# A recurrent layer's group norm without its mean: value weight and first states centred once, and the instruction order of four engines rewritten

## What is computed

```python
xa = _ln(x, ln1_w, ln1_b)
...
r = (xr @ Wr.T).reshape(b, l, h, s_)
k = (xk @ Wk.T).reshape(b, l, h, s_)
v = (xv @ Wv.T).reshape(b, l, h, s_)
g = jax.nn.silu(xg @ Wg.T)
s0 = state[:, 2:2 + s_].reshape(b, h, s_, s_)

def step(s, rkvw):
    r_t, k_t, v_t, w_t = rkvw
    a = k_t[..., :, None] * v_t[..., None, :]
    out = jnp.einsum('bhi,bhij->bhj', r_t, u * a + s)
    s = a + w_t[..., :, None] * s
    return (s, out)
...
og = out.reshape(b, l, h, s_)
m = og.mean(-1, keepdims=True)
va = ((og - m) ** 2).mean(-1, keepdims=True)
og = ((og - m) / jnp.sqrt(va + 1e-05)).reshape(b, l, e) * gn_w + gn_b
x1 = x + og * g @ Wo.T
xc = _ln(x1, ln2_w, ln2_b)
...
return x1 + rr * (kk @ Wfv.T)
```

## Time and profile before

| | |
|---|---|
| median of 3 runs | 4187.91 us (4187.29 to 4189.38) |
| the profiled execution | 4184.89 us, span 4183.2 us |
| the second layer in its span | first load issued at 648.59, last product of the output 1618.31 to 1619.00 |
| first scan, last scan | 727.78 and 1546.4 us |
| one sample in the steady part | 105.8 us, from the start of one variance matmul (L1222) to the next: 946.94, 1052.77, 1158.60, 1264.40, 1370.20 |
| busy in such a stretch | PE 104.20, PEld 78.30, DVE 93.23, ACT 32.80, POOL 63.76 us |
| granted clock of TensorE in it | 1.00 |

### The profile page before, as it was taken

How to read it: one execution, slowest core, us unless ns; L and a number is a source line. 1 busy time by engine, 2 the same in 40 slices (tenths; PEclk the granted TensorE clock), 3 DMA queues, 4 the chain that set the end, 5 groups by cost and what they waited for, 6 DMA issues and landing times. The chain is left out here.

```text
span 4183.2 us, 68211 instructions
## 1 busy us (share of the span) xinstructions
PE 3942.0 (94%) x20652; PEld 2981.3 (71%) x20652; DVE 2936.5 (70%) x6449; ACT 1925.5 (46%) x3836; POOL 1598.0 (38%) x1100
## 2 busy tenths in 40 slices
PE   7999996799999987999999999999999999999989
PEld 3333334567777755888977888877988877978866
DVE  6766652888888874767767767757767757767653
ACT  4666661233333323555543555533545534555522
POOL 1443432555666641332344332344332344333240
PEclk8999997999999998999999999999999999999999
DMA  5444423000000002222223222223121122122122
GB/s 169 127 129 131 132 61 127 11 6 16 16 16 16 11 11 84 72 66 77 64 66 109 62 75 72 64 74 104 58 90 57 61 79 90 61 92 70 54 79 98
DMA packets 159993, 298.64 MB, mean 71 GB/s; under 512 B 19780, under 2 KB 42820, under 8 KB 158544
## 3 DMA queue, kind: packets, MB, share of 16 engines
q1 hardware_dynamic: 157720, 291.12, 22.4%
q0 software_dynamic: 1008, 3.67, 0.2%
q10 hardware_dynamic: 1032, 0.97, 0.1%
HBM read 254.28 MB, written 42.21 MB: 71 GB/s over the span
## 5 line engine op out<-in xcount | busy, mean ns | idle before, releaser
L2220 POOL TENSOR_TENSOR c_wl<-c_wr,c_wh 128x512 fp32r<-128x512 f32 (+1 forms) x576 | 820.0, 1435 | 1606.1 <-ACT c_wh L2600 1368.1
L2701 ACT ACTIVATE c_pr<-c_ps,c_nms 128x257 f32<-128x257 f32 x512 | 244.2, 477 | 475.4 <-DVE c_nms L2940 473.1
L1741 DVE TENSOR_TENSOR_SCAN b_sb<-b_wt,b_s,b_ps 128x256 f32<-128x256 f32 x512 | 361.7, 736 | 15.6 <-PE b_ps L1194 3.1
L843 DVE TENSOR_REDUCE a_nm<-a_ps 128x2 f32<-128x1024 f32 x256 | 312.0, 1223 | 69.1 <-PE a_ps L490 68.4
L1692 POOL TENSOR_TENSOR b_sb<-b_sb,b_rt 128x1024 f32<-128x1024 f32 x128 | 277.8, 2177 | 156.2 <-DVE b_sb L1741 115.9
L2600 ACT ACTIVATE c_wh<-c_wr 128x512 fp32r<-128x512 f32 (+1 forms) x464 | 315.5, 688 | 45.8 <-PE c_ps L2307 41.9
L686 ACT ACTIVATE a_ex<-a_ps 128x1024 f32<-128x1024 f32 x256 | 260.6, 1022 | 147.2 <-PE a_ps L510 145.0
L2305 PE MATMUL c_ps<-c_hh,c_wh 128*128 128x512 f32 x768 | 307.4, 400 | 7.3 <-DVE c_hl L2806 7.3
L2305 PE MATMUL c_ps<-c_gh,c_wh 128*128 128x512 f32 x768 | 307.5, 400 | 6.2 <-DVE c_gl L3003 2.9
L2307 PE MATMUL c_ps<-c_hh,c_wl 128*128 128x512 f32 x768 | 304.4, 396 | 0.0
L2306 PE MATMUL c_ps<-c_hl,c_wh 128*128 128x512 f32 x768 | 304.1, 396 | 0.0
(11 more groups left out here) (379 smaller groups left out, 9985.4 us busy)
## 6 DMA issues: line engine op xcount, KB each, us to landing
c_wr<-in_downs SPq DMA_DIRECT2D x192, 256.0 KB, 2.6
c_wr<-in_wv SPq DMA_DIRECT2D x64, 512.0 KB, 4.0
c_wr<-in_wk SPq DMA_DIRECT2D x128, 256.0 KB, 2.9
c_wr<-in_wq SPq DMA_DIRECT2D x128, 256.0 KB, 2.6
a_qp<-strips SPq DMA_DIRECT2D x64, 256.0 KB, 4.5
a_kp<-strips SPq DMA_DIRECT2D x64, 256.0 KB, 4.5
c_wr<-in_fc SPq DMA_DIRECT2D x64, 256.0 KB, 2.8
strips<-a_qh SPq DMA_DIRECT2D x32, 256.0 KB
```

The lines of the kernel that those rows point to most:

```text
L843: dve.tensor_reduce(NM[:, s, :].rearrange("p (h c) -> p h c", h=HG)[:, 2 * p:2 * p + 2, c:c + 1], ps[:, bank:bank + 2, :], AX.X, ALU.max, ...
L1741: mm = dve.tensor_tensor_scan(SB[:, quad % RING, pr % 2, e, 1:L + 1], WT[:, third(b, i), e, :], half(spread_bank(pair), e), S0[:, b % 2, 2 ...
L2220: pool.tensor_tensor(piece(WL, slot), piece(WR, slot), piece(WH, slot), ALU.subtract).then_inc(piece_cut[slot], 1)
L2701: act.activation(PR[:, i, 0:L + 1], ps[:, BS + 1 - i % 2, 0:L + 1], ACT.Exp, bias=NMS[:, i:i + 1], scale=float(K2) ** -0.5, accum_out=RS[: ...
```

## The change

The weights of v and the first states get their mean over j taken out once, in the prologue, by VectorE (`center`); then `out` has no mean over j, and the two mean matmul groups, their subtractions, `BM` and the semaphores between them go, in the steady part and in the tail. The square now waits for the scans' sums themselves (`og_ready`). `S0` is loaded whole, for all 8 samples, by one transfer of 256 KB ahead of the later weights, in place of eight of 32 KB. The four tables are other ones throughout, and the products have a slot each.

```diff
-            for dst, src in ((SELF, selv), (SELG[:, :, :], selg), (BO[:, 0, :], blk[0]), (BM[:, :], blk[1]), (BMC[:, :, :], bmc), (BB[:, :, :], bb)):
+            for dst, src in ((SELF, selv), (SELG[:, :, :], selg), (BO[:, 0, :], blk), (BMC[:, :, :], bmc), (BB[:, :, :], bb)):
                 sp.dma_start(dst, src).then_inc(consts_in, 16)
-            sp.dma_start(S0[:, 0], s0[0]).then_inc(s0_in[0], 16)
+            sp.dma_start(S0[:, :, :, :], s0).then_inc(s0_in, 16)
...
-                    if t > 1:
-                        sp.wait_ge(s_ready, (t - 1) * PAIRS1 + AHEAD)
-                        sp.wait_ge(first_in, (t - 1) * QUADS + AHEAD)
-                    sp.dma_start(S0[:, t % 2], s0[t]).then_inc(s0_in[t % 2], 16)
...
                                 if t == 0:
-                                    pe.wait_ge(weights_in[w], 16)
+                                    if w == W_V:
+                                        pe.wait_ge(wv_centered, 1 + AHEAD)
+                                    else:
+                                        pe.wait_ge(weights_in[w], 16)
...
-                for i in range(2):
-                    s = due_post(slot, PE_AT["gm"][i])
-                    if s is not None:
-                        pe.wait_ge(og_ready, s * 2 + i + 1 + AHEAD)
-                        if i == 0:
-                            pe.wait_ge(fv_read, s * 2 + AHEAD)
-                        else:
-                            pe.wait_ge(gc_ready, s * 2 + 1 + AHEAD)
-                        for c in range(2 * i, 2 * i + 2):
-                            mm = pe.matmul(half(PB, c), BM[:, :], OG[:, s % 2, c, :], start=True, stop=True, skip_group_check=True)
-                        mm.then_inc(gm_ps, 1)
                 s = due_post(slot, PE_AT["gv"])
                 if s is not None:
                     pe.wait_ge(gq_ready, s + 1 + AHEAD)
-                    pe.wait_ge(gc_ready, s * 2 + 2 + AHEAD)
+                    pe.wait_ge(fv_read, s * 2 + AHEAD)
...
-                    act.wait_ge(gc_ready, s * 2 + 2 + AHEAD)
+                    act.wait_ge(og_ready, s * 2 + 2 + AHEAD)
...
+            def center():
+
+                dve.wait_ge(s0_in, 16 + AHEAD)
+                states = S0[:, :, :, :].rearrange("p b c j -> p (b c) j")
+                dve.tensor_reduce(SDB[:, 0:B * EC], states, AX.X, ALU.add)
+                dve.drain()
+                dve.scalar_tensor_tensor(states, SDB[:, 0:B * EC].unsqueeze(2).broadcast_to([P, B * EC, S1]), -1.0 / S1, states, ALU.mult, ALU.add).then_inc(s0_centered, 1)
+                dve.wait_ge(weights_in[W_V], 16)
+                sums = SDB[:, P:2 * P].rearrange("p (c h) -> p c h", h=HC1)
+                dve.tensor_reduce(sums, W[:, W_V].rearrange("p k (o j h) -> p (k o) h j", o=EC, h=HC1), AX.X, ALU.add)
+                dve.drain()
+                dve.tensor_scalar(sums, sums, 1.0 / S1, None, ALU.mult)
+                dve.drain()
+                columns = W[:, W_V].rearrange("p k (o j h) -> p (k o) j h", o=EC, h=HC1)
+                dve.tensor_tensor(columns, columns, sums.unsqueeze(2).broadcast_to([P, EC * EC, S1, HC1]), ALU.subtract).then_inc(wv_centered, 1)
...
+                            if t == 0 and e == 2 and i == 0:
+                                center()
...
-                for i in range(2):
-                    s = due_post(slot, DVE_AT["gm"][i])
-                    if s is not None:
-                        dve.wait_ge(gm_ps, s * 2 + i + 1 + AHEAD)
-                        dve.tensor_tensor(OG[:, s % 2, 2 * i:2 * i + 2, :], OG[:, s % 2, 2 * i:2 * i + 2, :],
-                                          both(PB), ALU.subtract).then_inc(gc_ready, 1)
...
-                    b = due(slot, 4 * pr + DVE_AT["multiply"])
+                    b = due(slot, DVE_AT["multiply"][pr])
```

More of the change, by code:

```diff
@@ L1099, in layer1 @@
         U_K, U_R, U_TW1, U_TW2, U_BONUS, U_V, U_G, UNITS = 0, 2, 4, 5, 7, 9, 11, 13
[L1100 to L1109, removed]
-                       mix=(-123, -121, -104, -71, -57), rk=(-111, -100), gate=-39, gated=143, scale2=166, shift2=188)
@@ L1111, in layer1 @@
-        DVE_AT = dict(multiply=-1, sums=(79, 148), mean=-111, inverse=-102, blend=-92, mix=(-81, -78, -73, -70, -56, -53, -42, -35, -29, -22),
-                      v=(-19, -11), gm=(168, 171), ginverse=182, bb=(184, 186), wo=(203, 209), mean2=213, inverse2=219, fkin=234, frin=239,
-                      fv=(283, 292), out=312)
-        FIRST, LAST = -188, B * SLOTS + 320
+        PE_AT = dict(mean=-158, var=-155, hidden=-122, mix=(-119, -114, -109, -102, -97, -92, -71, -66, -64, -61), k=(-105, -99), r=(-96, -86),
+                     tw1=-75, tw2=(-70, -65), bonus=(-64, -62), v=(-57, -51), g=(-46, -43),
+                     spread=(-46, -45, -43, -41, -39, -38, -32, -26, -23, -13, -5, 5, 6, 9, 12, 14, 18, 20, 29, 30, 34, 39, 40, 46, 53, 58, 63, 71, 72, 75, 76, 80),
+                     gather=(-12, 6, 15, 41, 58, 65, 83, 95), gv=137, bb=(148, 152), wo=(161, 168), mean2=169, var2=180, fk=(203, 207),
+                     fr=(219, 228), fv=(243, 253))
@@ new lines, in layer1 @@
+        ACT_AT = dict(square=-133, root=-111, norm=-106, hidden=-104, k=(-82, -70), r=(-69, -51), tw1=-47, tw2=(-46, -44), bonus=(-43, -42),
+                      v=(-40, -37), g=(-31, -16), states=(-14, -13, 10, 12, 21, 35, 47, 48, 58, 59, 61, 76, 82, 92, 93, 94), gsquare=147, groot=174,
+                      gnorm=175, square2=193, root2=207, norm2=214, fk=(217, 231), fr=(242, 256))
+        POOL_AT = dict(scale=-181, shift=-178, mix=(-162, -157, -126, -105, -98), rk=(-127, -106), gate=-73,
+                       weigh=(-69, -68, -58, -51, -42, -40, -2, 0, 1, 3, 19, 23, 31, 32, 34, 44), gated=113, scale2=149, shift2=158)
@@ L1116, in layer1 @@
+        DVE_AT = dict(mean=-109, inverse=-100, blend=-87, mix=(-76, -74, -73, -68, -62, -50, -33, -31, -28, -25), v=(-20, -12),
+                      multiply=(-4, -1, 4, 9, 12, 14, 17, 27, 29, 30, 33, 43, 44, 49, 56, 58, 62, 63, 64, 75, 76, 79, 80, 90, 96, 98, 99, 106, 110, 115, 116, 123),
+                      sums=(86, 150), ginverse=183, bb=(184, 187), wo=(202, 207), mean2=211, inverse2=218, fkin=233, frin=237, fv=(286, 299), out=311)
+        FIRST, LAST = -189, B * SLOTS + 320
         stack.callback(nc.all_engine_barrier)
@@ L1389, in last_stages @@
                 pe.wait_ge(mix_read, B * 10 + AHEAD)
-                for i in range(2):
-                    pe.wait_ge(og_ready, s * 2 + i + 1 + AHEAD)
-                    for c in range(2 * i, 2 * i + 2):
-                        mm = pe.matmul(half(LAST_BANKS[i], c), BM[:, :], OG[:, s % 2, c, :], start=True, stop=True, skip_group_check=True)
-                    mm.then_inc(gm_ps, 1)
                 pe.wait_ge(tr_ready, r * 2 + 1 + AHEAD)
```

36 lines of the change are left out of this document (14 added, 22 removed).

## The result

The changed kernel takes 4237.69 us (median of 4 runs, 4231.16 to 4238.75) against 4187.6 before: ratio 1.0118, 95% interval 1.0106 to 1.0131. It is slower by 50 us. The profiled execution has a span of 4237.2 us. From the first matmul of the second layer to the end of its last row lie 966.6 us before (652.35 to 1619.0) and 1021.7 after (654.97 to 1676.7): 55 us, so the loss is in this layer. The layer starts 2.6 us later and the third layer gives about 4 back (experiment 9 comes to it).

What follows compares the result with a forecast made beforehand. TensorE, nearly always streaming and coupled to VectorE by round trips, was taken as the bound; seven samples 16.8, first scans 1.4 + 1 and tail 1.8 sum to 21 us off 4187.9, so 4167 us, range 4150 to 4183.

Steps and rivals of the forecast that it cites:

- the one on VectorE's load: Steady samples: two subtractions, their wait and cheaper products cut VectorE's work by 3.95 us a sample, 4.2% of 93.2.
- Slower: Rival, chance 0.06: in the ring from gate to hidden layer, GpSimd reaches scale or shift with weighings under way; 4203 us.
- a hidden layer that waits over 2 us: Sign at the hidden layer in a sample, named as one that would show the prediction wrong.
- the 1.25 us: Steady samples: TensorE waits 1.25 us less for scans and mixes, between 0 and 2.0, giving 103.4 us a sample.
- TensorE's mean groups: Group norm's mean in each sample: two groups of 0.8 us go, and the variance's 0.55 us wait with them.
- my stretch: From one sample's gate to the next one's hidden layer: 24.4 us, bounds 23.7 and 25.1, hidden layer waiting about 0.7.
- the rival that VectorE was the bound: Rival, chance 0.18: all VectorE savings come through, 4.9 us a sample, 40 us with the ends; 4148 us.
- The centring: Prologue, once: 6.4 us of VectorE rows, making the next mix 2.7 us late, costed at 0.
- The cover: Prologue: TensorE asks for the late mix only behind tw1, which comes out within half a microsecond; 2.7 us if it fails.
- First scans: Start of the layer: a product and a scan fit into VectorE's second wait, 1.4 us, plus 1 us for the products' lead.
- The tail: Layer's end: two mean groups ahead of the fr half, which the square waits for, go; 1.8 us.

Runs made afterwards that it cites:

- experiment 9: The changed code with the order of the kernel before, the centring's rows spread in pieces over four VectorE waits in the prologue; 4167.6 us, ratio 0.9951 to before.
- experiment 2: The changed kernel with GpSimd held after each of the two shifts until VectorE's blend or first feed-forward mix is done; 4187.5 us, ratio 1.0002 to before.
- experiment 5: The changed kernel with GpSimd held only after the first shift until VectorE's blend is through, nothing held at the mix; 4217.4 us, ratio 1.0070 to before.
- experiment 1: The changed code with the four tables of the kernel before, mean entries left out, centring in one piece; 4180.9 us, ratio 0.9986 to before.
- experiment 4: The kernel before with one edit, every product half a pair earlier (slot 4 pr - 3 in place of 4 pr - 1); 4238.0 us, ratio 1.0121 to before.
- experiment 8: The changed kernel with GpSimd held at both blend and mix, and every product directly ahead of its own scans; 4193.2 us, ratio 1.0016 to before.
- experiment 6: The kernel before with one weighing of GpSimd put behind the shift in place of ahead of it; 4221.6 us, ratio 1.0082 to before.
- experiment 7: The changed kernel, nothing held, each blend row reading one SBUF tensor in place of two (result differs); 4230.8 us, ratio 1.0104 to before.

## Why the prediction was wrong

**The step that failed** is the one on VectorE's load: "So its work falls by 1.35 + 2.6 = 3.95 us a sample". It takes every duration from a row of before and lets the order move rows without changing them. In the changed order VectorE's rows grew by 1.9 (blend) and 3.8 us (mix), since GpSimd had a row ready in the moment when its shift released them, and by 1.5 (output sum) beside an addition; the sum's growth cost nothing that the runs show. The prediction looked for GpSimd in the chain only as the engine that comes late with the scale or the shift ("Slower"), and there it found one weighing in both orders, rightly. It did not ask what GpSimd starts **behind** the shift. The order's rows have it: ahead of the change nothing was ready there, with it weighings and an addition were. Experiments 2 and 5 put 50 and 20 us on it. The mark that I had named, "a hidden layer that waits over 2 us", came true (2.66).

**A second step, the 1.25 us.** Without the collisions (experiment 2) the time is that of before, so the forecast would have failed without them too. The term that fails there is "what TensorE stops waiting", taken as 1.25 between bounds of 0 and 2.0. The 2.0 was read from the waits of TensorE's weight loads, and weight loads run beside matmuls. The matmuls' own waits in before, over four samples, are:

```profile
PE b_ps L1232 <- DVEq L1776: 2.5, 4, 0.6
PE b_ps L1304 <- ACT b_sqb L1530: 2.2, 4, 0.6
PE b_ps L1183 <- DVE b_sb L1741: 1.1, 4, 0.3
```

For the scans that is 1.1 us where the loads show 5.3, and for the mixes nothing where they show 3.4. A sample of 105.8 has 1.6 us in which TensorE is idle; less the two waits that the prediction treats apart (0.63 and 0.55) about 0.4 was left to save, not 2.0.

**The clock.** I priced no wait above its own length. Of the 7.0 us, 3.2 are matmuls at half clock behind waits of 2.6 us; the waits of 1.5 in experiment 1 have no such rows, and in experiment 4 some waits of 2.77 have them and some do not. Without them the change would have cost about 28 us (50 less 7 times 3.2; an estimate).

**TensorE's mean groups.** Right in size and worth less: its busy time fell by 1.4 us a sample (104.2 to 102.8), "about 1.5" was forecast, and the variance of the group norm no longer waits. But the sample shrank only by 0.9 in the old order, since the wait for the blend grew from 0.63 to 1.5; my stretch had 0.7. In the new order, collisions removed, it shrank by 0.1, where 2.4 were forecast: all of TensorE's waits together came to 3.0 us (105.75 less 102.8), more than the 1.6 of before: 0.8 at the blend, 0.7 at the v half, and four of 0.3 to 0.4 at mixes and projections.

**VectorE's lighter load.** It came, smaller than the 3.95: two subtractions less took the busy time from 93.2 to 92.1 us (experiment 1), and the lead took another 1.7 (experiments 2 and 8, without the output sum's growth); in experiment 4 the lead took 2.0 (93.2 to 91.2). No sample got shorter by it: with and without the lead a steady sample takes 105.75 and 105.6 us. So the rival that VectorE was the bound is not borne out either. In all the lead is worth perhaps 5.7 us in the new order, and minus 8 in the old one.

**The centring.** Sized at 6.4 us, measured 7.8 (694.85 to the next mix at 702.67), with 3.86 for the strided sum in place of 2.4, inside the doubt that I had allowed. Costed at 0, it cost 7.3 in the old order. The cover named was that TensorE asks for the late mix only behind tw1; in the changed kernel tw1 itself waits for the addition that the late mix feeds, and its rows then run at half clock. tw1 starts 50.7 us after the layer's first matmul, 0.8 later than before, and the row behind it 2.6 later:

```profile
705.65 3.68 PE L1264 MATMUL b_ps<-b_xf,b_tw 128*64 128x256 f32 x8 [3.50 <-POOL b_xf L1633]
```

**First scans.** Forecast 1.4 + 1 us sooner; the first came 88.4 us after the first matmul, 12.9 later than before. About 7 are the centring's, by the measure of experiment 1. The rest is here: the second product stands ahead of the first scan, and waits.

```profile
735.93 0.69 DVE L1723 TENSOR_TENSOR b_ps<-b_kt,b_ps 128x512 f32<-128x512 f32 x1 [0.19 <-issue]
742.74 0.70 DVE L1723 TENSOR_TENSOR b_ps<-b_kt,b_ps 128x512 f32<-128x512 f32 x1 [6.12 <-PE b_ps L1177]
743.34 1.38 DVE L1737 TENSOR_TENSOR_SCAN b_sb<-b_wt,b_s,b_ps 128x256 f32<-128x256 f32 x2
```

It is the same mistake as in experiment 4: I counted what a lead saves and not what waits behind it. In experiment 8, without the lead, the first scan comes after 82.4 us. The 6 us are not on the path, though: the third blend comes 215.3 us after the first matmul there and 214.8 in experiment 2.

**The tail.** Forecast 1.8; from the last of the mixes L1843 in its first form (1534.7 before) to the layer's end it is 2.3 us shorter than before in experiment 2 and 3.1 in experiment 1, and no shorter in the changed kernel.

So the new order without its collisions is no better than the old one before the change: it loses 14 us up to the third blend and gives back 7 in the samples and the tail. The centring is about 7 of the 14; 6 more are lost from the second blend to the third, where TensorE is busy for 80.5 us at a granted clock of 0.84, against 74.9 at 0.90 before. The edit itself, the centring, gains when its rows lie in VectorE's waits.

## What to carry to other kernels

When an order is moved, look at pairs of engines and not only at queues: for each VectorE row with both inputs in SBUF, or a fast single-input one, look at what GpSimd starts in the moment that releases it. A releasing row (here the shift) is the likeliest place, because its engine is free right then. And a row moved ahead of its time is only free of cost if its own input is there; ask what stands behind it. One-time work belongs into waits in pieces, not in front of one row.

## What the runs showed of the hardware

A VectorE row of 0.47 us became 2.38 us beside a GpSimd row of 2.17, and a GpSimd row of 2.18 us took 3.10 when an output sum on VectorE joined it, which itself took 2.67 in place of 1.22; a reciprocal, rows with an input in PSUM and sums of one tensor beside GpSimd kept their length and did not lengthen GpSimd's rows. A `tensor_scalar` with one SBUF input was locked out as well (0.34 to 2.25 us), which I had not expected. Behind waits of 2.2 to 3.8 us on TensorE the granted clock mostly fell to half for some of the next matmuls, in the changed kernel and in experiments 4 to 7, which added 1.5 to 3 us to such a wait; in experiment 4 two of the waits of 2.77 us in the steady part were followed by none. A strided sum of 512 elements took 1.03 us (4.1 for four, 3.86 in one piece of 2048), where the sum of the states, 512 in a row, took 0.67.
